# W2's Walsh-Hadamard transform: two more butterfly stages on GpSimd, and gates as one activation, in a mixer and gated FFN

## The chip, the cores and the metric

The kernel runs on one core of a Trainium2 chip. A core has TensorE (PE in the profile; PEld is its weight load), VectorE (DVE), ScalarE (ACT), GpSimd (POOL) and SyncE (SP, which here issues all DMAs). The metric is device microseconds of one execution, as the median of the runs. Before the change it is 731.81 us, the median of 3 runs from 729.76 to 732.04.

## The reference, cut to what matters

Input x is 4 blocks (batch) of 512 tokens of 512 values, float32.

```python
def attn(x, Wi, Wf, Wg, Wo, gnorm_w):          # weights 512 x 512
    i, f, g = x @ Wi.T, x @ Wf.T, x @ Wg.T
    gate = sigmoid(f)
    v = silu(i) * (1 - gate)
    o = scan over tokens of  o[t] = gate[t] * o[t-1] + v[t]
    o = o * rsqrt(mean(o*o) + 1e-5) * gnorm_w * silu(g)
    return o @ Wo.T
def ffn(x, W1, W2, W3):                        # W1, W3: 2048 x 512, W2: 512 x 2048
    hidden = silu(x @ W1.T) * (x @ W3.T)
    hidden = fwht(hidden)                      # Walsh-Hadamard over 2048, / sqrt(2048)
    return hidden @ W2.T
x = x + layernorm(attn(layernorm(x), ...))
x = x + layernorm(ffn(layernorm(x), ...))
```

## The kernel before, in words

The transform is put on W2 once, and not on the hidden values of each block: 2048 is 16 chunks of 128, so the transform is a 128 x 128 Hadamard product inside each chunk and a 16-point butterfly (four stages) across the chunks. W2 comes in 8 units of 64 output columns; a unit is 128 partitions x 16 chunks x 64 float32. GpSimd does three of the four stages (`FW.m.k`, unit m, k from 0 to 5: two instructions of 128x512 a stage, one for the sums and one for the differences, L1393 to L1407), going back and forth between the unit's place and a spare buffer (`unit_tmp`: x1r, gate or a half of ot, which units share in turn, so that a unit waits until TensorE has read the one before it in the same buffer). The fourth stage is on TensorE: for each half unit (`H2.m.h`, L746 to L756) two float32 products of 128 x 512 accumulate, with the Hadamard matrix and, for the second half, with its negative. A float32 product of this kind stands in the trace as two matmul records. ACT copies the bank to a float16 high half (L982), VectorE writes the float16 low half (L1298). All large products are of this kind: float16 high and low halves in three passes (`three_passes`, L580 to L582).

The work of a block b: `XT` transposes of the normed input; `F`, `I`, `G` projections (4 chunks c each; 12 matmuls of 512 columns a chunk); gates (below); the scan on VectorE (`S`, L1135 to L1144); squares of o summed on GpSimd (`S` there, L1373); low halves of the gated o on GpSimd (`P`, L1378); `MS` mean squares and `Y` output projection (4 tiles) on TensorE; norm, add, second norm (`YN`, `Z1`, `Z2`); `ZT` transposes; the FFN; the down projection `D.b.0` to `D.b.63` (chunk and token tile, three matmuls of 512 each); final norm `V` and `W`. Block 0's FFN is 16 chunks of `GA` and `UP` products (12 matmuls each). Blocks 1 to 3 use a scheme of seven products for a 2 x 2 grid in place of eight (`GP`, `GQ`, `GR`, `GU`, with `combine` steps on VectorE), whose sums of weights are made in blocks 0 and 1: raw weights are loaded (`SL`), summed by four GpSimd instructions (`SA`, L1419 to L1428), split (`SH` on ACT, `SO` on VectorE, L1246) and stored (`SS`); the next chunk of raw weights is loaded only when the last one is split.

A gate is a sigmoid on ACT, and then, for a silu, a product with the argument on VectorE: `I` L1132, `G` L1149, `GA` L1317. Then `UP` multiplies by the linear part (L1329), ACT makes the high half (L1009) and GpSimd the low half (`UP` there, L1432), which frees the buffer (`sga`, two deep) for the next-but-one gate.

What each engine does next is written out by hand in five lists: PE_ORDER (with the PSUM bank behind each colon), ACT_ORDER, DVE_ORDER, POOL_ORDER and SP_ORDER; each engine takes its list strictly in order, and semaphores make it wait for the others. The first down step waits for all low halves of W2 (`h2_lo`, L821).

## Time and profile before

| | us |
|---|---|
| median of 3 runs | 731.81 (729.76 to 732.04) |
| the profiled execution | 732.31 |
| its span, first to last instruction | 730.5 |
| TensorE busy | 702.2 (96%) |
| VectorE busy | 524.1 (72%) |
| GpSimd busy | 319.2 (44%) |
| ScalarE busy | 279.7 (38%) |
| mean granted TensorE clock | 0.988 |

Busy time is the union of an engine's instructions. Matmuls are pipelined, so how long one record is says less than how far apart two of them start. The full clock is 2.4 GHz and stands as 1.00; the lower level, 1.2 GHz, as 0.50. In a row of the timeline the first two numbers are the start and the length in us, then engine, line, operation, what it writes and reads, shape and count; in brackets the idle time before it and what ended that.

### The profile page before, as it was taken

How to read it: one execution, taken by the hardware profiler on the slowest of the kernel's cores; microseconds unless marked ns; L12 is line 12 of the kernel's file. 1: busy time of each engine (PE TensorE's matmuls, PEld its weight loads, DVE VectorE, ACT ScalarE, POOL GpSimd, SP SyncE). 2: the span in 40 equal slices, each digit the busy share in tenths (PEclk: the TensorE clock that was granted, in tenths of full speed). 3: DMA queues.
4: the chain of work that ended last, by engine and by line, in shares of the span. 5: the costliest groups of instructions: out<-in, count | busy, mean ns of one | idle time of the engine just before them, and what ended most of it. 6: DMA issues, size and time to landing. Idle time of an engine off the chain costs nothing.

```text
span 730.5 us, 11286 instructions
## 1 busy us (share of the span) xinstructions
PE 702.2 (96%) x4280; PEld 428.7 (59%) x4280; DVE 524.1 (72%) x873; ACT 279.7 (38%) x450; POOL 319.2 (44%) x268
## 2 busy tenths in 40 slices
...
GB/s 321 404 318 0 174 44 75 102 184 116 153 107 130 258 174 98 238 213 128 119 201 117 102 260 100 36 154 145 100 100 112 146 150 61 143 287 102 32 1 87
DMA packets 28199, 105.73 MB, mean 145 GB/s; under 512 B 2800, under 2 KB 7152, under 8 KB 23536
## 3 DMA queue, kind: packets, MB, share of 16 engines
...
HBM read 81.92 MB, written 23.07 MB: 144 GB/s over the span
## 4 chain that ended last, share of the span: by engine, by line
PE 69%; POOL 13%; DVE 7%; DMA 5%; issue 3%; ACT 2%; DVEq 1%; SPq 0%; POOLq 0%; ACTq 0%
PE ps L580 22%; PE ps L581 22%; PE ps L582 22%; DMA ring<-W13t 3%; DVE ring L1246 2%; POOL w2t L1407 2%; POOL ot L1407 2%; POOL ring L1432 1%; POOL ring L1422 1%; DMA ring<-L_attn_Wf 1%; POOL ring L1424 1%; POOL res L1417 1%; PE ps L722 1%; POOL x1r L1407 1%; POOL ring L1426 1%
## 5 line engine op out<-in xcount | busy, mean ns | idle before, releaser
L580 PE MATMUL ps<-xb,ring 128*128 128x256 f16 (+1 forms) x704 | 225.9, 321 | 1.4 <-DVE ring L1090 1.4
L581 PE MATMUL ps<-xb,ring 128*128 128x256 f16 (+1 forms) x704 | 225.9, 321 | 0.0
L582 PE MATMUL ps<-xb,ring 128*128 128x256 f16 (+1 forms) x704 | 225.9, 321 | 0.0
L1360 POOL TENSOR_TENSOR rstd<-var,neg_half 128x1 f32<-128x1 f32 x64 | 45.9, 718 | 120.7 <-DVE var L1338 55.1
L580 PEld LDWEIGHTS ps<-xb,ring 128*128 128x128 f16 x704 | 69.0, 98 | 48.2 <-issue 3.1
L581 PEld LDWEIGHTS ps<-xb,ring 128*128 128x128 f16 x704 | 68.9, 98 | 46.8 <-issue 1.7
L582 PEld LDWEIGHTS ps<-xb,ring 128*128 128x128 f16 x704 | 68.9, 98 | 42.1
L582 PE MATMUL ps<-ring 128*128 128x256 f16 x288 | 78.5, 273 | 0.0
L581 PE MATMUL ps<-ring 128*128 128x256 f16 x288 | 78.5, 273 | 0.0
L580 PE MATMUL ps<-ring 128*128 128x256 f16 x288 | 78.5, 273 | 0.0
L1432 POOL TENSOR_TENSOR ring<-sga,ring 128x512 f16<-128x512 f32 x36 | 45.6, 1280 | 71.7 <-ACT ring L1009 71.7
L1432 POOL TENSOR_TENSOR hsp<-sga,hsp 128x512 f16<-128x512 f32 x24 | 28.9, 1215 | 88.4 <-ACT hsp L1009 88.4
L1317 DVE SCALAR_TENSOR_TENSOR sga<-ring,gate_c,sga 128x512 f32<-128x512 f32 x48 | 41.1, 857 | 26.9 <-ACT sga L997 26.7
L976 ACT ACTIVATE junk<-ps 128x256 f32<-128x256 f32 x48 | 18.4, 383 | 96.7 <-PE ps L582 96.6
L580 PE MATMUL ps<-w2t,ring 128*128 128x512 f16 x144 | 54.6, 379 | 0.0
L581 PE MATMUL ps<-w2t,ring 128*128 128x512 f16 x144 | 54.6, 379 | 0.0
L582 PE MATMUL ps<-w2t,ring 128*128 128x512 f16 x144 | 54.6, 379 | 0.0
L997 ACT ACTIVATE sga<-ring,gate_c 128x512 f32<-128x512 f32 x48 | 34.6, 720 | 43.8 <-DVE ring L1281 35.3
L1270 DVE TENSOR_TENSOR ring<-ps,ring 128x512 f32<-128x512 f32 x48 | 33.0, 688 | 24.2 <-PE ps L582 23.7
L1281 DVE TENSOR_TENSOR ring<-ps,ring 128x512 f32<-128x512 f32 x48 | 33.1, 689 | 20.3 <-PE ps L582 19.5
L1260 DVE TENSOR_TENSOR ring<-ps,junk 128x512 f32<-128x512 f32 x48 | 33.1, 689 | 17.8 <-PE ps L582 15.0
L1378 POOL TENSOR_TENSOR ot<-sg,ot 128x512 f16<-128x512 f32 x16 | 22.4, 1397 | 50.9 <-ACT ot L916 50.9
...
## 6 DMA issues: line engine op xcount, KB each, us to landing
...
ring<-W13t SPq DMA_DIRECT2D x8, 1024.0 KB, 6.4
w_comb<-ring SPq DMA_DIRECT2D x8, 1024.0 KB, 8.5
...
w2t<-W2t SPq DMA_DIRECT2D x8, 512.0 KB, 11.6
...
```

The costliest lines, as they stand in the source:

```text
L580: pe.matmul(dst, a_hi, b_hi, start=start, stop=False)
L581: pe.matmul(dst, a_hi, b_lo, start=False, stop=False)
L582: return pe.matmul(dst, a_lo, b_hi, start=False, stop=stop)
L997: act.activation(sga[:, c % 2], src, ACT.Sigmoid, scale=gate_c[:]).then_inc(sga_rdy, 1)
L1260: dve.tensor_tensor(combined(g % 2)[:, 0:512].rearrange("p (o t) -> p o t", o=2), bank("GQ", b, g)[:].rearrange("p (o t) -> p o t", o=2), ...
L1270: dve.tensor_tensor(to[:, 512:1024].rearrange("p (o t) -> p o t", o=2), bank("GR", b, g)[:].rearrange("p (o t) -> p o t", o=2), both, ALU. ...
L1281: dve.tensor_tensor(to[:, 512:1024], bank("GU", b, g)[:], to[:, 512:1024], ALU.add).then_inc(gu_rdy, 1)
L1317: dve.scalar_tensor_tensor(sga[:, c % 2], src, gate_c[:], sga[:, c % 2], ALU.mult, ALU.mult).then_inc(sil_rdy, 1)
L1360: pool.tensor_tensor(dst, src, neg_half[:].broadcast_to(src.shape), ALU.pow).then_inc(done, 1)
L1378: pool.tensor_tensor(ot[:, 1, c, :], sg[:], ot[:, 0, c, :], ALU.subtract).then_inc(o_lo, 1)
L1407: pool.tensor_tensor(to, a, b, op).then_inc(w2_fly, 1)
L1432: pool.tensor_tensor(hid(b, c, 1), sga[:, c % 2], hid(b, c, 0), ALU.subtract).then_inc(hid_lo, 1)
```

## The change: what it does

1. All four stages of W2's butterfly run on GpSimd: 8 instructions a unit and not 6 (64, not 48, in all). They end in the unit's own place, with one spare buffer (x1r) for all units, and `FW` waits only for its own earlier steps. Each half unit is one product with the Hadamard matrix; the negative matrix and its step `HN` go. ACT's copy of a half now waits for both products of the unit, since its target overlaps their source. The first loads of x1r on SP wait for the last butterfly.
2. i, g and the FFN's gates are one Silu activation; the products on VectorE (`I`, `G`, `GA`) go, and the gain's coefficient goes into `P`, which becomes a scalar_tensor_tensor. The forget gate is 0.5 * tanh(f / 2) + 0.5: a Tanh and then an Identity on ACT. PSUM banks of `GA`, `I`, `G` are free after the activation.
3. Some small VectorE steps take another form: scalar_tensor_tensor on 128x1 becomes tensor_scalar, and three on 128x2 become pairs of 128x1.
4. All five order lists are new.

```diff
@@ butterflies and their product
-        def unit_tmp(m):
...
-        UNIT_TMP = ("x1r", "gate", "x1r", "ot0", "ot1", "gate", "x1r", "ot0")
...
+        unit_tmp = x1r[:].rearrange("p s d -> p (s d)").rearrange("p (c d) -> p c d", d=UW)
...
-            src, dst = (unit_raw(m), unit_tmp(m)) if stage % 2 == 0 else (unit_tmp(m), unit_raw(m))
+            src, dst = (unit_raw(m), unit_tmp) if stage % 2 == 0 else (unit_tmp, unit_raw(m))
...
-                pe.wait_ge(w2_fly, 6 * (m + 1))
...
-                pe.matmul(bank("H2", m, h)[:], had[:], low, start=True, stop=False)
-                pe.matmul(bank("H2", m, h)[:], neg_had[:] if h else had[:], high, start=False, stop=True
-                          ).then_inc(h2_mm, 1)
+                pe.wait_ge(w2_fly, 8 * (m + 1))
+                chunks = unit_raw(m)[:, HC // 2 * h:HC // 2 * (h + 1), :].rearrange("p c d -> p (c d)")
+                pe.matmul(bank("H2", m, h)[:], had[:], chunks, start=True, stop=True).then_inc(h2_mm, 1)
...
-                act.wait_ge(h2_mm, 2 * m + h + 1)
+                act.wait_ge(h2_mm, 2 * m + 2)
...
-                    sp.wait_ge(h2_mm, 2 * UNITS)
+                    sp.wait_ge(w2_fly, 8 * UNITS)
...
-                    if UNIT_TMP[m] == "gate":
-                        pool.wait_ge(o_rdy, KC)
-                    if UNIT_TMP[m] in ("ot0", "ot1"):
-                        pool.wait_ge(y_mm, TC)
-                    if unit_before(m) is not None:
-                        pool.wait_ge(h2_mm, 2 * (unit_before(m) + 1))
+                    if m > 0:
+                        pool.wait_ge(w2_fly, 8 * m)
@@ gates
-                act.activation(gate[:, c % 2], bank("F", b, c)[:], ACT.Sigmoid, scale=unscale[:, 0:1]
+                act.activation(gate[:, c % 2], bank("F", b, c)[:], ACT.Tanh, scale=unscale[:, 0:1]
+                               ).then_inc(tanh_rdy, 1)
+                act.wait_ge(tanh_rdy, n + 1)
+                act.activation(gate[:, c % 2], gate[:, c % 2], ACT.Identity, bias=half[:], scale=0.5
                                ).then_inc(gate_rdy, 1)
...
-                act.activation(si[:], bank("I", b, c)[:], ACT.Sigmoid, scale=unscale[:, 1:2]
+                act.activation(si[:], bank("I", b, c)[:], ACT.Silu, scale=unscale[:, 1:2]
...
-                act.activation(sga[:, c % 2], src, ACT.Sigmoid, scale=gate_c[:]
+                act.activation(sga[:, c % 2], src, ACT.Silu, scale=gate_c[:]
...
-                dve.scalar_tensor_tensor(si[:], bank("I", b, c)[:], unscale[:, 1:2], si[:],
-                                         ALU.mult, ALU.mult).then_inc(sli_rdy, 1)
...
-                dve.scalar_tensor_tensor(sg[:], bank("G", b, c)[:], g_coef[:, c:c + 1], sg[:],
-                                         ALU.mult, ALU.mult).then_inc(gs_rdy, 1)
...
-                dve.tensor_tensor(sg[:], sg[:], o_s[:], ALU.mult).then_inc(op_rdy, 1)
+                dve.scalar_tensor_tensor(sg[:], sg[:], g_coef[:, c:c + 1], o_s[:], ALU.mult, ALU.mult).then_inc(op_rdy, 1)
...
-                dve.scalar_tensor_tensor(sga[:, c % 2], src, gate_c[:], sga[:, c % 2],
-                                         ALU.mult, ALU.mult).then_inc(sil_rdy, 1)
@@ a small step's form
-                dve.scalar_tensor_tensor(var[:, 1, t:t + 1], mv[:, 1, t, 1:2], y_inv[:, 1:2], ms_eps[:, t:t + 1],
-                                         ALU.mult, ALU.add).then_inc(y_var, 1)
+                dve.tensor_scalar(var[:, 1, t:t + 1], mv[:, 1, t, 1:2], y_inv[:, 1:2], ms_eps[:, t:t + 1],
+                                  ALU.mult, ALU.add).then_inc(y_var, 1)
```

Of the new lists, the parts around the edits. PE_ORDER (up to block 0's first gate products, and from its last ones to the down projection):

```
... I.0.3:0 W2N.0.0:3 ... W2N.7.0 W2S.0.0:2 H2.0.0:1 MS.0.0:4 H2.0.1:5 Y.0.0:6 Y.0.1:0 WS.0.0:7 Y.0.2:3 Y.0.3:2
ZT.0.0:4 ZT.0.1:1 ZT.0.2:5 ZT.0.3:7 H2.1.0:6 H2.1.1:0 GA.0.0:3 XT.1.0:2 UP.0.0:4 XT.1.1:1 XT.1.2:5 XT.1.3:7 ...
... GA.0.14:6 UP.0.14:3 GA.0.15:2 UP.0.15:4 MS.1.0:0 Y.1.0:5 Y.1.1:1 Y.1.2:7 Y.1.3:6 H2.2.0:3 H2.2.1:2 H2.3.0:4
H2.3.1:0 H2.4.0:5 H2.4.1:1 H2.5.0:3 H2.5.1:7 H2.6.0:2 H2.6.1:4 H2.7.0:0 H2.7.1:5 D.0.0 D.0.1 D.0.2 D.0.3 D.0.4
D.0.5 ZT.1.0:7 ZT.1.1:4 D.0.6 D.0.7 D.0.8 ZT.1.2:5 ...
```

In the list before, H2.2 and H2.3 stand among the gate products of chunks 2 and 3, H2.4 to H2.7 around UP.0.12 ahead of block 1's projections. ACT_ORDER at the end of block 0's attention:

```
... S.0.2 WN.2.0 I.0.3 WN.3.0 P.0.2 WN.4.0 G.0.3 S.0.3 WN.5.0 P.0.3 WN.6.0 H2.0.0 H2.0.1 WN.7.0 WT.0.0 ...
```

POOL_ORDER (FW of units 0 and 1; then the end of the butterflies):

```
... X1.0.3 FW.0.0 FW.0.1 P.0.0 P.0.1 S.0.1 S.0.2 FW.0.2 FW.0.3 FW.0.4 P.0.2 FW.0.5 FW.0.6 FW.0.7 S.0.3 P.0.3
FW.1.0 FW.1.1 FW.1.2 Y.0.0 FW.1.3 Y.0.1 FW.1.4 FW.1.5 Y.0.2 YN.0.0 YN.0.1 Y.0.3 Z1.0.0 YN.0.2 YN.0.3 Z1.0.1
FW.1.6 Z1.0.2 Z1.0.3 FW.1.7 FW.2.0 X1.1.0 ...
... FW.6.7 UP.0.12 SA.1.0 P.1.0 S.1.1 FW.7.0 FW.7.1 FW.7.2 FW.7.3 FW.7.4 P.1.1 FW.7.5 FW.7.6 FW.7.7 P.1.2 S.1.2
SA.2.0 P.1.3 S.1.3 UP.0.13 UP.0.14 S.2.0 UP.0.15 Y.1.0 YN.1.0 Y.1.1 Y.1.2 Z1.1.0 YN.1.1 Y.1.3 YN.1.2 Z1.1.1
SA.3.0 Z1.1.2 YN.1.3 ...
```

DVE_ORDER at the end of W2 and at the end of the kernel; SP_ORDER around block 1's first combined weights:

```
... H2.7.0 H2.7.1 YN.1.3 Z2.1.1 Z1.1.2 SO.3.0 Z2.1.2 Z1.1.3 Z2.1.3 ZT.1.0 ...
... V.3.0 V.3.1 W.3.0 W.3.1 V.3.2 V.3.3 W.3.2 W.3.3
... SL.2.0 SS.1.0 LR.0.0 LR.0.1 WL.1.0 SL.3.0 SS.2.0 ST.1.0 ...
```

## Rows read from the trace of the kernel before

**Rows 1.** The page, part 1: busy us, share of the span, instructions

```profile
PE 702.2 (96%) x4280; PEld 428.7 (59%) x4280; DVE 524.1 (72%) x873; ACT 279.7 (38%) x450; POOL 319.2 (44%) x268
```

**Rows 2.** Table by stage, all engines; columns: stage, its us, busy, granted clock, DMA

```profile
52.00:91.00 39.00, 30.37 (x155) 16.87 (x153) 27.22 (x62) 19.31 (x32) 31.23 (x29) 0.82 0.30 103
91.00:166.80 75.80, 75.80 (x345) 35.32 (x344) 70.93 (x89) 39.40 (x62) 69.92 (x49) 1.00 0.28 98
...
183.10:218.00 34.90, 33.84 (x157) 15.18 (x155) 26.89 (x26) 17.19 (x26) 24.43 (x15) 1.00 0.41 135
...
248.00:260.00 12.00, 11.42 (x63) 5.95 (x62) 8.96 (x10) 6.38 (x11) 10.84 (x9) 1.00 0.63 209
260.00:724.00 464.00, 464.00 (x3200) 314.58 (x3198) 315.07 (x536) 140.06 (x234) 138.35 (x127) 1.00 0.37 131
```

**Rows 3.** Table by stage, GpSimd alone, then its butterflies (L1407) alone

```profile
84.00:216.00 132.00, 109.85 (x77) 0.98 0.36 122
...
84.00:216.00 132.00, 56.98 (x38) 0.98 0.36 122
```

**Rows 4.** Timeline of TensorE: output projection, transposes, Hadamard products, gate products, mean squares

```profile
59.79 0.59 PE L580 MATMUL ps<-ring,ot 128*128 128x512 f16 x1
...
81.45 1.09 PE L632 MATMUL ps<-ident,rows 128*128 128x128 f32 x4 [5.34 <-DVE rows L1186]
...
86.43 1.99 PE L754 MATMUL ps<-gate,had 128*128 128x512 f32 x2
...
90.83 0.38 PE L580 MATMUL ps<-xb,ring 128*128 128x512 f16 x1
...
166.78 1.02 PE L754 MATMUL ps<-ot,had 128*128 128x512 f32 x2
...
170.22 0.38 PE L580 MATMUL ps<-xb,ring 128*128 128x512 f16 x1
...
172.81 1.02 PE L754 MATMUL ps<-gate,had 128*128 128x512 f32 x2
...
218.10 1.02 PE L689 MATMUL ps<-ones,osum 128*128 128x1 f32 x8 [1.16 <-POOL osum L1373]
```

**Rows 5.** Timeline of GpSimd: the last add of squares, blocks 0 and 1

```profile
54.75 1.71 POOL L1373 TENSOR_TENSOR osum<-osum,osq 128x512 f32<-128x512 f32 x1
...
215.72 2.24 POOL L1373 TENSOR_TENSOR osum<-osum,osq 128x512 f32<-128x512 f32 x1
```

**Rows 6.** Line L1407, 84 to 216 us: least, median, greatest ns of one

```profile
L1407 POOL TENSOR_TENSOR x1r<-w2t x8: 1263/1714/1720, 86.2 to 149.5; 128x512 f32<-128x512 f32 x8
```

**Rows 7.** Groups by line: count, busy us, mean ns of one, idle before

```profile
L1317 DVE SCALAR_TENSOR_TENSOR sga<-ring,gate_c,sga 128x512 f32<-128x512 f32 x48 | 41.1, 857 | 26.9 <-ACT sga L997 26.7
L947 ACT ACTIVATE junk<-ring 128x1024 bf16<-128x1024 f32 x16 | 16.8, 1051 | 0.4
L1149 DVE SCALAR_TENSOR_TENSOR sg<-ps,g_coef,sg 128x512 f32<-128x512 f32 x16 | 11.8, 737 | 5.6 <-ACT sg L904 5.5
L1298 DVE SCALAR_TENSOR_TENSOR w2t<-ps,w_s,w2t 128x512 f16<-128x512 f32 x16 | 11.6, 746 | 5.6 <-ACT w2t L982 5.6
L1424 POOL TENSOR_TENSOR ring<-ring 128x512 f32<-128x512 f32 x8 | 10.8, 1350 | 0.6
L1338 DVE TENSOR_SCALAR var<-mv,v_inv 128x1 f32<-128x1 f32 x16 | 3.4, 214 | 0.7 <-DVE mv L1053 0.2
```

**Rows 8.** Timeline of VectorE: small steps of the first output norms

```profile
71.85 1.27 DVE L1167 SCALAR_TENSOR_TENSOR var<-mv,y_inv,ms_eps 128x1 f32<-128x1 f32 x1
...
73.29 0.16 DVE L1175 SCALAR_TENSOR_TENSOR ab<-mv,ysc 128x1 f32<-128x1 f32 x1
```

**Rows 9.** The page, part 6: DMA issues, KB each, us to landing

```profile
ring<-W13t SPq DMA_DIRECT2D x8, 1024.0 KB, 6.4
```

**Rows 10.** Timeline of ScalarE: the table load

```profile
0.73 1.28 ACT L839 ACT_TABLE_LOAD   x1 [0.73 <-PEq L1451]
```

**Rows 11.** The chain that ended last, its end

```profile
724.29 2.84 DMA x1r<-x_rows
```

More of the change, by code:

```diff
@@ L167 @@
[L167 to L171 removed]
+S.0.0 X1.0.0 X1.0.1 X1.0.2 X1.0.3 FW.0.0 FW.0.1 P.0.0 P.0.1 S.0.1 S.0.2 FW.0.2 FW.0.3 FW.0.4 P.0.2 FW.0.5 FW.0.6
@@ L213, in mixer_ffn_kernel @@
         neg_half = sb("neg_half", [P, 1])
+        half = sb("half", [P, 1])
         warm = sb("warm", [P, 1])
@@ L837, in _ @@
         def _(act):
-            act.wait_ge(half_set, 1)
-            act.activation(warm[:], neg_half[:], ACT.Sigmoid)
+            act.wait_ge(half_set, 2)
+            act.activation(warm[:], neg_half[:], ACT.Silu)
             def xt(b, t):
@@ L903, in g @@
                     act.wait_ge(o_lo, n)
-                act.activation(sg[:], bank("G", b, c)[:], ACT.Sigmoid, scale=unscale[:, 2:3]
+                act.activation(sg[:], bank("G", b, c)[:], ACT.Silu, scale=unscale[:, 2:3]
                                ).then_inc(sgg_rdy, 1)
@@ L1026, in _ @@
         def _(dve):
+            dve.memset(half[:], 0.5).then_inc(half_set, 1)
             dve.memset(neg_half[:], -0.5).then_inc(half_set, 1)
```

358 lines of the change are left out of this document (165 added, 193 removed).

## The prediction

> **What bounds the kernel now.** I read the page's busy shares first, then a table by stage, then TensorE's own order of time where the table shows a hole, then GpSimd the same way. TensorE is busy 96% of the span [rows 1]. A busy share says little by itself, because matmuls are pipelined, so look at the stages [rows 2]: from 91 to 166.8 us it is busy for 75.80 of 75.80 us, from 260 to 724 us for 464.00 of 464.00, at the full granted clock (1.00). In between it loses 1.1 us (183.1 to 218) and 0.6 (248 to 260). Only before 91 us are there real holes, 8.6 of 39 us at a granted clock of 0.82. So from the first gate product (90.83 us) to 724 us the time is TensorE's work plus 1.7 us, and an edit there counts only if it takes work from TensorE or makes it wait.
>
> The edge beside it is GpSimd from 84 to 216 us: busy for 109.85 of 132 us [rows 3]. It holds W2's butterflies, the hidden values' low halves, the sums of weights, and the low halves and squares of block 1's attention. The one wait of TensorE in that stage, 1.16 us in front of the mean squares at 218.10, ends with GpSimd's last add of squares (start 215.72) [rows 4, 5]. GpSimd has 22 us of slack there, and the change gives it more work. VectorE is at 70.93 of 75.80 us from 91 to 166.8 [rows 2], but nothing on TensorE waits for it.
>
> **1. One Hadamard product a half unit: TensorE.** Each half unit has two float32 products now, each of two records. Eight records take from 166.78 to 170.22, so 0.43 us each [rows 4]. Half of 64 records go: 32 x 0.43 = 13.7 us. They aren't worth the same. Unit 0's 1.7 us lie ahead of a hole of 5.34 us (the transposes at 81.45 wait for the rows) and are worth nothing. Unit 1's (86.43 to 90.83, part of it at half clock) lie between the transposes and the first gate product. Those of units 2 to 7, 24 records, 10.3 us, lie in the full stretch and come off whole: **-10.3 us**.
>
> **2. Two more butterflies a unit: GpSimd.** 16 instructions more. Mean of one now, 84 to 216 us: 56.98 / 38 = 1.50 us [rows 3]; the ends are 1.26 and 1.72 [rows 6]. That is 24 us, 20 to 27.5. What it costs depends on the cover, in three places.
>
> *(a) The front.* The new list puts five of unit 0's butterflies between the adds of squares 2 and 3, three of them right before the last; now only one stands there. Now the last add ends at 56.5 [rows 5] and the output projection starts at 59.79 [rows 4]. In the new ACT list each piece of weight squares (two passes of 1.05 us, some 2.3 us with their readings [rows 7]) precedes one of the last gates: WN.2, I, WN.3, P.0.2, WN.4, G.0.3, S.0.3, WN.5, P.0.3. From 48 us, where I put the first of them, I count 4 x 2.3 + 5 x 0.65 and 1.2 of waiting for the last I product = 13.7, so the last low half of o is there at about 62 + 1.3 = 63; Y starts near 64.5, not 59.8, but with unit 0's products already done. The stage's granted clock is 0.82 [rows 2]: part of it runs at 1.2 GHz and not 2.4, after TensorE had waited, and an output tile that falls there takes up to twice its 2.59 us. I put 2 us of that into Y here. Then Y.0.3 ends near 76; now it is 72.5 (81.45 less the hole of 5.34 and unit 0's products of 3.4). From there norm, add and second norm take until the transposes end at 86.4, 14 us, and in them small VectorE operations wait up to 1.27 us, where 0.16 is normal [rows 8]. The new forms (one scalar operand fewer, L1167 and L1175) don't need that wait if they behave as L1338, 0.21 on the mean of 16 [rows 7]. With three of four tiles already on their way I take 10 us for it: last transposes at 86, unit 1 then 1.7 to 3.4 us, **first gate product at 89.3, not 90.83: -1.5 us** (bounds 86.5 and 94).
>
> The Trainium skill ("SBUF — State Buffer", Who interferes with whom) has a rule for this: a VectorE operation with two inputs in SBUF and a GpSimd operation that reads SBUF exclude each other for a whole instruction. The trace agrees for the small operations (1.27 us against 0.16). By that rule added butterflies would also slow VectorE's weight splits; VectorE loses more work than that (part 3).
>
> *(b) 84 to 216 us.* By 86.3 us (unit 1's last butterfly as I count it) the new list has done 16 butterflies, the old one 10 by 84. So 10 of the 16 fall into the stage: 10 x 1.50 = +15.0. Of the sums of weights only three chunks, not four, stand ahead of the last add of squares: four instructions less, of some 1.35 to 1.43 (L1424 [rows 7]; I take 1.35) = -5.4. So 109.85 + 15.0 - 5.4 = 119.5 us from 86.3 on, end 205.8; with 2.5 us for waits that remain (now 22; the list puts its work in another order, and a chunk of raw weights lands 6.4 us after its issue [rows 9]) 208.3. TensorE has before the mean squares: 32 gate and up products and 12 projections, 44 x 2.59 (170.22 to 172.81 is one [rows 4]), and four short transposes and a little: 115.8, from 89.3 to 205.1. It waits 3.2 us where it now waits 1.2: **+2.0 us**. Bounds: no wait (-1.2) and, with nothing absorbed in the front and 1.72 each, 109.85 + 27.5 - 5.4 + 86.3 + 2.5 = 220.8, a wait of 15.7 (+14.5). I take the mean of the stage because the same 32 weight splits run beside GpSimd as now, and what comes on top runs after them, near 1.26.
>
> *(c) Units 2 to 7 in one piece before the down projection.* Now they stand among gate products. In the new list D.0.0 stands right behind H2.7.1 and waits for its copy on ACT (about the same 0.7) and its low half on VectorE (0.75 [rows 7]), with two handovers: **+1.7 us** (0.9 to 4; VectorE needs 0.75 a bank and TensorE will need 0.86, so it just keeps up). Behind it on VectorE and ACT stand block 1's last norm steps and one chunk of weight sums (two instructions on VectorE), while TensorE has 9 down steps (5.8 us) and two transposes before it needs the last norm: I put 1.6 us of waiting, against the 0.6 lost there now [rows 2]: **+1.0 us** (0 to 4).
>
> **3. Gates as one activation.** VectorE loses the multiplications by the argument: 48 x 0.86 and three sets of 16 x 0.74 = 77 us [rows 7]; P changes form, which I price at nothing. ACT keeps its number for i, g and the FFN gates and gains one 0.6 us step for each of 16 forget gates, 10 us on an engine 38% busy [rows 1]. In the full stretch nothing waits for these 77 us, so they are worth **0**; they shorten hand-offs and free banks sooner, which makes the stretch from 260 to 724 us safer. Behind a forget gate's extra step stands the scan, 0.6 us a chunk; in the front that is inside (a).
>
> **4. SP, POOL and the end.** The first two loads of x1r wait for the last butterfly instead of the last product; both come long before their use in block 0's final norm. In SP's list the first combined weights are asked for earlier and wait for the last up product (near 205), and raw chunk 3 queues behind; its sums are first read by block 1's combined products. The last order on VectorE is W.3.0 W.3.1 V.3.2, so W.3.1 and its load of x1r (issued at 724.29 now, a wait of 2.84 us [rows 11]) come one norm earlier: **-0.7 us**.
>
> Sum: -1.5 - 10.3 + 2.0 + 1.7 + 1.0 - 0.7 = **-7.8 us**. The profiled execution took 732.31 us (span 730.5, 1.8 around it), so 724.5; it stands 0.5 over the median of the runs (731.81), so **724.0** for the median.
>
> **The rivals.**
> 1. *TensorE keeps all it gains.* GpSimd is through before 205 us and the last units hide their copies. For it: 22 us of slack [rows 3], butterflies of 1.26 after the splits. Against: the order on GpSimd puts a chunk of sums (5.4 us) before the last P and S. -1.5 - 10.3 - 1.2 - 0.7 = -13.7: **718.1**.
> 2. *GpSimd becomes the bound up to the mean squares* (the other side). Place: S.1.3 at the end of its list. Price: each us past 205.1 is one of TensorE. It eats the gain once GpSimd ends 11 us after TensorE gets there (216), so at 119.5 + 8 us of work or waits. At the upper bound of (b): -7.8 + 12.5 = +4.7, **736.5**. For it: TensorE already ends its wait at 218 on just that instruction. Against: butterflies moved ahead of 86 us.
> 3. *The full stretch leaks.* Orders laid out anew put pairs of products in bunches over four banks; 0.03 us at each of their 144 bank hand-overs, or five waits of 1 us, make +5: **729**. For it: now 464.00 of 464.00, which can only get worse. Against: VectorE has 48 x 0.86 us less in just these hand-overs.
> 4. *The tables switch.* If Tanh and Silu aren't loaded together, each forget gate needs two loads, 32 x 1.28 = 41 us on ACT, of which block 0's 8 (10 us) lie on the path and the rest beside TensorE's work: -7.8 + 10 and some waits, **736**. The skill's page gives 2.66 us a switch with its drain; by that figure, an estimate, it would be 21 us.
>
> **How the numbers follow.** Forecast 0.47, rival 1 0.26, rival 2 0.13, rival 3 0.11, rival 4 0.03. A change under 0.3% (2.2 us: 729.6 to 734.0) can't be told from none here. Faster: 0.47 + 0.26 + 0.05 of rival 3 = 0.78. Same: 0.05 of rival 2, 0.05 of 3 = 0.10. Slower: 0.08 + 0.01 + 0.03 = 0.12. The likeliest one's own range is 721 to 728; to hold 8 in 10 it reaches from just under rival 1 to the near half of rivals 2 and 3: 716.5 to 730.
>
> **What would show it.** Step 1: 32 records on the line of the Hadamard product, none on a second. (a): the first gate product between 88 and 91 us, Y from about 64. (b): GpSimd's last add of block 1 near 208 and a wait of TensorE of 2 to 5 us before the mean squares; no wait makes rival 1, over 10 us rival 2. (c): a hole of 1 to 2.5 us between the last Hadamard product and the first down step. Step 3: one table load and no more; over 260 to 724 us TensorE busy throughout. Wrong would be the whole argument if the end moves by more than TensorE's work plus the holes of its own timeline.

## The result and the profile after

The changed kernel takes 736.38 us (median of 5 runs, 735.30 to 737.85) where the kernel before takes 731.81 (729.76 to 732.04). The ratio is 1.0072, 95% interval 1.0050 to 1.0094: slower, by 0.7%. I had forecast 724.0 (716.5 to 730). Of all executions here only one is far from its median: one of the six of e13_front_and_fill took 1883.9 us, and its ratio leaves that one out.

The page of after, part 1, beside [rows 1]; columns as there:

```profile
PE 692.5 (94%) x4248; PEld 424.9 (58%) x4248; DVE 463.1 (63%) x781; ACT 291.6 (40%) x466; POOL 335.4 (46%) x284
```

TensorE has lost 32 instructions, as the change says. VectorE has lost 61 us, and not the 77 of my step 3. The span is 734.6 us, 4.1 more than before: TensorE does less and waits longer. Where, the table by stage says (columns as in [rows 2]):

```profile
52.00:91.00 39.00, 23.09 (x105) 12.80 (x102) 23.23 (x63) 21.42 (x37) 31.93 (x29) 0.73 0.15 51
91.00:166.80 75.80, 75.51 (x350) 35.07 (x349) 68.01 (x75) 37.84 (x59) 72.25 (x52) 0.98 0.34 113
...
183.10:218.00 34.90, 27.95 (x131) 12.69 (x128) 22.36 (x14) 15.99 (x24) 34.19 (x24) 0.93 0.38 128
218.00:232.00 14.00, 14.00 (x57) 6.81 (x57) 8.61 (x21) 2.17 (x4) 8.15 (x8) 0.81 0.54 169
232.00:248.00 16.00, 13.58 (x41) 5.83 (x40) 15.21 (x29) 11.67 (x17) 10.77 (x11) 1.00 0.09 34
...
260.00:728.00 468.00, 468.00 (x3221) 316.47 (x3219) 266.48 (x476) 148.56 (x245) 138.32 (x131) 1.00 0.38 134
```

From 260 us on TensorE is busy for 468.00 of 468.00, as before. From 183.1 to 218 it is busy for 27.95 of 34.9 where it was 33.84, and GpSimd, which had 24.43 us of work there, has 34.19. TensorE's timeline of after names the waits (start, us, engine, line, operation, and in brackets the idle time ahead and its releaser):

```profile
83.77 1.09 PE L617 MATMUL ps<-ident,rows 128*128 128x128 f32 x4 [5.24 <-DVE rows L1154]
88.64 3.01 PE L617 MATMUL ps<-ident,rows 128*128 128x128 f32 x12 [3.79 <-DVE rows L1154]
91.45 2.89 PE L737 MATMUL ps<-w2t,had 128*128 128x512 f32 x4
94.28 0.38 PE L565 MATMUL ps<-xb,ring 128*128 128x512 f16 x1
...
217.69 1.84 PE L674 MATMUL ps<-ones,osum 128*128 128x1 f32 x8 [6.95 <-POOL osum L1338]
219.39 0.59 PE L565 MATMUL ps<-ring,ot 128*128 128x512 f16 x1
...
244.49 0.38 PE L565 MATMUL ps<-w2t,hsp 128*128 128x512 f16 x1 [2.42 <-DVE w2t L1274]
...
252.32 0.63 PE L707 MATMUL ps<-ident,rows 128*128 128x128 f32 x4 [0.97 <-DVE rows L1154]
```

The 1.16 us in front of block 1's mean squares [rows 4] have become 6.95, and the releaser is the same: GpSimd's last add of squares. The wait costs more than itself, since the granted clock is down behind it; the same line read in two windows (stage, TensorE busy, granted clock, DMA):

```profile
212.94:223.18 10.24, 5.49 (x17) 0.50 0.50 165
223.18:226.00 2.82, 2.82 (x15) 1.00 0.94 286
```

0.50 is 1.2 GHz, 1.00 is 2.4. The mean squares and the first output tile lie in the slow window and take 1.7 and 4.4 us where they take 0.9 and 2.6 at full clock: 2.6 us more. GpSimd's timeline shows what it did ahead of that add:

```profile
190.61 2.25 POOL L1368 TENSOR_TENSOR x1r<-w2t 128x512 f32<-128x512 f32 x1
...
202.98 2.82 POOL L1368 TENSOR_TENSOR w2t<-x1r 128x512 f32<-128x512 f32 x2
205.76 1.60 POOL L1343 TENSOR_TENSOR ot<-sg,ot 128x512 f16<-128x512 f32 x1
207.33 2.18 POOL L1338 TENSOR_TENSOR osum<-osum,osq 128x512 f32<-128x512 f32 x1
209.47 1.71 POOL L1383 TENSOR_TENSOR ring<-ring 128x512 f32<-128x512 f32 x1
...
215.16 1.16 POOL L1343 TENSOR_TENSOR ot<-sg,ot 128x512 f16<-128x512 f32 x1
216.28 1.27 POOL L1338 TENSOR_TENSOR osum<-osum,osq 128x512 f32<-128x512 f32 x1
```

It hardly ever pauses: of the 34.90 us from 183.1 to 218 it is busy for 34.19. Counted from the end of unit 1's last butterfly to the end of that add, all of GpSimd and then its butterflies alone:

```profile
90.15:217.55 127.40, 122.85 (x85) 0.97 0.36 122
...
90.15:217.55 127.40, 75.57 (x48) 0.97 0.36 122
```

The queue is also one half of a chain through other engines: the last two `G` gates of block 1 on ScalarE wait for GpSimd's low half before them, and VectorE's product waits for the first of these gates:

```profile
201.77 0.69 ACT L886 ACTIVATE sg<-ps,unscale 128x512 f32<-128x512 f32 x1 [1.61 <-POOL ot L1343]
...
202.49 0.96 DVE L1124 SCALAR_TENSOR_TENSOR sg<-sg,g_coef,o_s 128x512 f32<-128x512 f32 x1 [2.99 <-ACT sg L886]
...
207.46 0.69 ACT L886 ACTIVATE sg<-ps,unscale 128x512 f32<-128x512 f32 x1 [2.77 <-POOL ot L1343]
```

TensorE's last record, before and after:

```profile
723.96 0.38 PE L582 MATMUL ps<-w2t,xb 128*128 128x512 f16 x1
```

```profile
728.43 0.38 PE L567 MATMUL ps<-w2t,xb 128*128 128x512 f16 x1
```

The groups by line of after (count, busy us, mean ns), and for the weight splits (L1216) the same group of before (L1240), which [rows 7] does not hold:

```profile
L1368 POOL TENSOR_TENSOR w2t<-x1r 128x512 f32<-128x512 f32 x32 | 49.2, 1556 | 3.2 <-PE ps L722 2.4
L1368 POOL TENSOR_TENSOR x1r<-w2t 128x512 f32<-128x512 f32 x32 | 48.5, 1531 | 22.9 <-DMA w2t<-W2t 21.8
L1216 DVE SCALAR_TENSOR_TENSOR ring<-ring,w_s 128x512 f16<-128x512 f32 x32 | 48.1, 1557 | 0.0
...
L1135 DVE TENSOR_SCALAR var<-mv,y_inv,ms_eps 128x1 f32<-128x1 f32 x16 | 4.4, 273 | 0.8 <-DVE mv L1034 0.2
```

```profile
L1240 DVE SCALAR_TENSOR_TENSOR ring<-ring,w_s 128x512 f16<-128x512 f32 x32 | 41.2, 1308 | 0.0
```

### The profile page after: what moved, and what is told of

Read it like the earlier page. It is cut to its first block, busy times and chain, and to the rows that moved or that the text cites. A ratio compares the mean times of both kernels' runs of the same rounds, so it can differ in the third digit from the quotient of the medians.

```text
span 734.6 us, 11163 instructions
## 1 busy us (share of the span) xinstructions
PE 692.5 (94%) x4248; PEld 424.9 (58%) x4248; DVE 463.1 (63%) x781; ACT 291.6 (40%) x466; POOL 335.4 (46%) x284
## 4 chain that ended last, share of the span: by engine, by line
PE 73%; POOL 11%; DVE 11%; issue 2%; DMA 1%; DVEq 1%; ACT 0%; SPq 0%; POOLq 0%
PE ps L565 23%; PE ps L566 23%; PE ps L567 23%; DVE ring L1216 5%; POOL w2t L1368 3%; POOL x1r L1368 2%; PE ps L707 1%; POOL ring L1393 1%; POOL rstd L1325 1%; DVEq L1033 1%; POOL ring L1389 1%; POOL ring L1383 1%; DVE sga L1294 1%; PE ps L617 1%; POOL ring L1387 1%
## 5 line engine op out<-in xcount | busy, mean ns | idle before, releaser
L1325 POOL TENSOR_TENSOR rstd<-var,neg_half 128x1 f32<-128x1 f32 x64 | 42.9, 672 | 98.9 <-DVE var L1303 29.8
L567 PE MATMUL ps<-ring 128*128 128x256 f16 x288 | 78.5, 273 | 0.0
L566 PE MATMUL ps<-ring 128*128 128x256 f16 x288 | 78.5, 273 | 0.0
L565 PE MATMUL ps<-ring 128*128 128x256 f16 x288 | 78.5, 273 | 0.0
L1368 POOL TENSOR_TENSOR x1r<-w2t 128x512 f32<-128x512 f32 x32 | 48.5, 1531 | 22.9 <-DMA w2t<-W2t 21.8
L1294 DVE SCALAR_TENSOR_TENSOR sga<-ring,up_c,sga 128x512 f32<-128x512 f32 x48 | 39.2, 820 | 24.2 <-ACT sga L977 22.3
L1368 POOL TENSOR_TENSOR w2t<-x1r 128x512 f32<-128x512 f32 x32 | 49.2, 1556 | 3.2 <-PE ps L722 2.4
L1216 DVE SCALAR_TENSOR_TENSOR ring<-ring,w_s 128x512 f16<-128x512 f32 x32 | 48.1, 1557 | 0.0
```

What stands on the lines that cost most here:

```text
L565: pe.matmul(dst, a_hi, b_hi, start=start, stop=False)
L566: pe.matmul(dst, a_hi, b_lo, start=False, stop=False)
L567: return pe.matmul(dst, a_lo, b_hi, start=False, stop=stop)
L1216: dve.scalar_tensor_tensor(ffn_w(c)[:, w, 1], ffn_raw(c)[:, w], w_s[:, w:w + 1], ffn_w(c)[:, w, 0], ALU.mult, ALU.subtract).then_inc(wt_lo, 1)
L1294: dve.scalar_tensor_tensor(sga[:, c % 2], src, up_c[:], sga[:, c % 2], ALU.mult, ALU.mult).then_inc(hid_rdy, 1)
L1325: pool.tensor_tensor(dst, src, neg_half[:].broadcast_to(src.shape), ALU.pow).then_inc(done, 1)
```

## The experiments

All were run beside the kernel before. Ratio to it, with its 95% interval; the last two columns are TensorE's start, in each profile, of block 1's mean squares and of the first down product (left empty for e4, whose order of TensorE is that of before).

| kernel | us | ratio | mean squares | first down |
|---|---|---|---|---|
| after | 736.38 | 1.0072 (1.0050 to 1.0094) | 217.7 | 244.5 |
| e1_pool_swap | 735.48 | 1.0052 (1.0037 to 1.0066) | 214.9 | 243.0 |
| e2_h2_in_hole | 736.27 | 1.0061 (1.0045 to 1.0077) | 222.2 | 233.4 |
| e3_small_last | 724.94 | 0.9909 (0.9891 to 0.9926) | 209.0 | 233.1 |
| e4_gates_alone | 732.89 | 1.0024 (1.0010 to 1.0038) | | |
| e5_middle | 755.68 | 1.0333 (1.0309 to 1.0358) | 215.4 | 251.9 |
| e6_front | 742.17 | 1.0148 (1.0121 to 1.0175) | 224.6 | 251.5 |
| e7_both | 759.34 | 1.0386 (1.0361 to 1.0412) | 219.8 | 256.3 |
| e8_swap_clean | 739.39 | 1.0112 (1.0097 to 1.0128) | 216.3 | 248.2 |
| e9_swap_fill | 736.81 | 1.0083 (1.0069 to 1.0097) | 214.8 | 243.2 |
| e10_attention_first | 734.64 | 1.0061 (1.0048 to 1.0074) | 211.2 | 242.6 |
| e11_sums_back | 734.20 | 1.0042 (1.0028 to 1.0056) | 212.0 | 236.1 |
| e12_sums_late | 732.46 | 1.0020 (1.0010 to 1.0030) | 211.4 | 235.4 |
| e13_front_and_fill | 737.32 | 1.0089 (1.0065 to 1.0112) | 215.7 | 237.4 |
| e14_front_norm | 738.04 | 1.0094 (1.0073 to 1.0114) | 217.7 | 245.2 |

**Is it GpSimd's work?** e3_small_last:

```diff
+            if stage == 3:
+                return d[:, :, half, 0:64], s[:, :, 0, 0:64], s[:, :, 1, 0:64], ALU.subtract if half else ALU.add
```

> The kernel after with the fourth butterfly stage computed on 64 of the 512 elements of each partition (seven eighths of that stage are left out); the number of instructions and all orders stay. It takes away GpSimd's time for 16 of the 64 butterflies' halves, some 16 x 1.3 = 21 us, 14 of them ahead of the mean squares. Theory A (GpSimd's added work costs the result): the wait ahead of the mean squares goes (7.1 us), with it the half clock (2.6), and a part of the front's 3.5: 9 to 13 us off, 723.5 to 727.5. Theory B (it is the order of the steps, not GpSimd's work): under 3 us, 733.5 to 736.5.

724.94 us, 11.4 under after. No order was touched, and TensorE now meets its square in time; TensorE's mean squares, GpSimd's last add, the shortened butterflies and VectorE's splits in its trace:

```profile
208.98 1.02 PE L676 MATMUL ps<-ones,osum 128*128 128x1 f32 x8
...
207.57 1.27 POOL L1340 TENSOR_TENSOR osum<-osum,osq 128x512 f32<-128x512 f32 x1
...
L1370 POOL TENSOR_TENSOR w2t<-x1r 128x512 f32<-128x512 f32 x16 | 25.7, 1623 | 2.7 <-PE ps L724 2.4
L1370 POOL TENSOR_TENSOR w2t<-x1r 128x64 f32<-128x64 f32 x16 | 7.5, 484 | 0.5
...
L1218 DVE SCALAR_TENSOR_TENSOR ring<-ring,w_s 128x512 f16<-128x512 f32 x32 | 41.0, 1337 | 0.0
```

This is theory A. 8.7 us earlier at the mean squares and 2.6 of half clock make the 11.4. The splits are back at 1337 ns with nothing of theirs changed. The 0.9% under before is no kernel to keep, since most of a stage is missing; it shows what is left of the 10.3 us of step 1 where GpSimd isn't in the way, but the front (first gate product at 93.2 us, 90.83 before) and the wait at the first down product (2.42 us) still cost.

**Are the gates worth nothing?** e4_gates_alone is before with `ACT.Silu` for i, g and the FFN gates, and `ACT.Tanh` with `ACT.Identity, bias=half, scale=0.5` for f; VectorE's order without I, G and GA.

> The kernel before with its butterflies, products and orders, and only the gates changed to one activation each (Silu, and Tanh with a second step for the forget gate); VectorE's order loses the steps I, G and GA. Theory A (my step 3: VectorE's 77 us stand beside TensorE and are worth nothing): 731 to 733 (731.8 before). Theory B (they shorten the front and the last wait of the middle stage): up to 3 us off, 729. Theory C (the gates themselves cost, by the extra ScalarE step or by tables): 734 or more.

732.89 us, inside theory A's range, but by the interval 0.7 to 2.8 us over the kernel before that ran beside it (731.08). The gates are worth nothing, or cost up to 0.4%; where that little comes from stays open.

**Can TensorE's wait be ordered away?** e1 moves one chunk of sums behind the last low half and square, e2 puts ready Hadamard products into TensorE's wait:

```diff
-P.1.2 S.1.2 SA.2.0 P.1.3 S.1.3          (e1, POOL_ORDER)
+P.1.2 S.1.2 P.1.3 S.1.3 SA.2.0
-UP.0.15 MS.1.0 Y.1.0 ... Y.1.3 H2.2.0 ... H2.7.1   (e2, PE_ORDER, banks changed)
+UP.0.15 H2.2.0 ... H2.7.1 MS.1.0 Y.1.0 ... Y.1.3
```

> The kernel after with one step of GpSimd's order moved: SA.2.0, a chunk of weight sums of four instructions (5.7 us in the trace of after), stands behind the last two low halves and squares of block 1's attention and no longer ahead of them. Theory A (GpSimd is what TensorE waits for up to block 1's mean squares, and its order decides when): the mean squares at 217.7 us come at about 212.3, TensorE's wait of 7.1 us shrinks to 1.7, and the stretch at half clock behind it (1.2 GHz from 212.9 us, some 2.6 us more of TensorE) shrinks or goes: 5 to 8 us off, 728.5 to 731.5. Theory B (the loss sits elsewhere, in the front or in the down projection, and the wait only stands in for it): under 1.5 us, 735 to 736.5.

> The kernel after with the twelve Hadamard products of units 2 to 7 ahead of block 1's mean squares and output projection on TensorE instead of behind them (their copies and low halves on ScalarE and VectorE go with them, and the down products of block 0 are spread otherwise between the transposes that follow). GpSimd's order is untouched. Theory A (TensorE idles 7 us for GpSimd, and 10 us of ready work stood behind the wait): the wait at 210.6 us is filled, the clock stays up, and the bubble before the first down product (2.6 us) goes too: 9 to 11.5 us off, 725 to 727.5. Theory B (the units aren't ready any earlier, or what is gained is waited for again at the last norm of block 1): 0 to 4 us off, 732.5 to 736.5.

0.9 and 0.1 us, both theory B by the time. In e2 the first down product starts 11.1 us earlier, as forecast, and the gain is given back by 290 us. TensorE's wait and the step on VectorE that stands ahead of the norm it waits for:

```profile
252.81 1.09 PE L709 MATMUL ps<-ident,rows 128*128 128x128 f32 x4 [4.76 <-DVE rows L1156]
...
246.53 2.48 DVE L1224 SCALAR_TENSOR_TENSOR ring<-ring,w_s 128x1024 f16<-128x1024 f32 x2 [3.98 <-ACT ring L949]
```

VectorE is to write the norm's rows, and stands at a weight-sum step that waits for ScalarE, which waits for GpSimd. In e1 the mean squares came 2.8 us earlier and not 5.4: with the sums out of the way GpSimd stood idle for 2.41 us ahead of the last low half (212.38 us), which needs ScalarE's copy. Behind the mean squares the same weight-sum step stood on VectorE ahead of their reading (it waited 8.65 us, until 221.22), and the FFN's last gate came on ScalarE at 222.65 us, behind that chunk's split and the low half UP.0.13, both of which the swap had left late.

Two larger rearrangements, and both together, came out much worse. e5 moves the weight sums behind block 1's norm and puts units 2 and 3 ahead of the mean squares; e6 puts the output projection ahead of unit 0's products and GpSimd's last low halves and square ahead of unit 0's last butterflies, and so moves butterflies of units 0 and 1 back; e7 is both. Their orders for PE and POOL, cut:

```diff
-UP.0.15 MS.1.0 Y.1.0 ... Y.1.3 H2.2.0 ...        (e5, PE_ORDER, banks changed)
+UP.0.15 H2.2.0 H2.2.1 H2.3.0 H2.3.1 MS.1.0 Y.1.0 ... Y.1.3 H2.4.0 ...
-... Z1.1.1 SA.3.0 Z1.1.2 ... ZA.1.6 SA.4.0 X1.2.0 ...   (e5, POOL_ORDER)
+... Z1.1.1 Z1.1.2 ... ZA.1.6 SA.3.0 X1.2.0 ...
-FW.0.2 FW.0.3 FW.0.4 P.0.2 FW.0.5 FW.0.6 FW.0.7 S.0.3 P.0.3 FW.1.0 FW.1.1 FW.1.2 Y.0.0 ...   (e6, POOL_ORDER)
+P.0.2 FW.0.2 FW.0.3 S.0.3 P.0.3 FW.0.4 FW.0.5 Y.0.0 FW.0.6 Y.0.1 FW.0.7 FW.1.0 Y.0.2 ...
```

> The kernel after with new orders in the middle only (front and all arithmetic as in after): units 2 and 3 ahead of block 1's mean squares on TensorE and units 4 to 7 behind the output projection; on GpSimd the last two low halves and squares ahead of a chunk of weight sums; the next chunks of weight sums behind block 1's norm and no longer inside it (VectorE's steps and the loads on SP with them); the down products of block 0 spread to match. Why: filling TensorE's wait alone gave nothing, because in that trace the norm of block 1 stood behind VectorE's step on the weight sums (it waited 4.0 us for GpSimd's) and TensorE then waited 4.9 us at the norm's transposes and 3.6 us at block 2's. Theory A (the loss is GpSimd's wait, and after it a second and third wait of the same kind, all three a matter of order): the first down product at 233.5 us and not 244.5, no wait over 1 us behind it: 11 to 12.5 us off, 723.5 to 726. Theory B (behind the two waits stands a third resource, such as VectorE at 12 to 13 of 14 us there): 3 to 8 us off, 728 to 733.

> The kernel after with new orders in the front only (up to 110 us): the output projection ahead of unit 0's Hadamard products, GpSimd's low half and squares of the last gates ahead of unit 0's last butterflies, ScalarE's copies of the last gates ahead of the weight squares, unit 1's products behind the first gate and up product. Theory A (GpSimd bounds the stretch up to the mean squares of block 1 whatever TensorE does ahead of it): the first gate product comes 6 to 8 us earlier (86 to 88 us, 94.3 in after), but the mean squares only 0 to 3 us, so 0 to 3 us off: 733 to 736. Theory B (the front's delay of 3.5 us over the kernel before goes straight into the end): 6 to 8 us off, 728 to 730.

> Both sets of orders together. Theory A: the middle's 11 us, and of the front's 6 to 8 us what GpSimd lets through. TensorE then comes to the mean squares near 208 us and GpSimd's last add of squares ends near 213: 720 to 723. Theory B of the front (all of it counts): 716.5 to 719. If the middle's orders only work because TensorE comes late to them: 725 or more.

All three lie above every range given for them but e7's last, which is open upwards. TensorE waits in e5 for 3.41 us behind the mean squares, for a gate on ScalarE that waits 7.97 us for UP.0.13 behind the sums on GpSimd; then 7.81 and 3.36 us at the Hadamard products and the first down product, where VectorE is late with its low halves behind two weight-sum steps (229.62 us, 3.48 long) and the norm; and 9.57 us in block 2, whose gates on ScalarE stand behind chunk 6 of the sums (GpSimd starts it at 314.2 us, 289.5 in after). e6 is the cleaner lesson: its first gate product came at 95.1 us, not at 86 to 88, and the mean squares 6.9 us later than in after. TensorE's wait there, and GpSimd from 90 us:

```profile
224.63 1.62 PE L677 MATMUL ps<-ones,osum 128*128 128x1 f32 x7 [9.29 <-POOL osum L1341]
...
90.00:224.00 134.00, 129.04 (x90) 0.95 0.35 116
```

Butterflies moved out of the front come back at the mean squares: theory A's mechanism, with a worse end than either theory had. The first gate product came 0.8 us later than in after, so this isn't a test of what an earlier TensorE would bring.

**Amount or place?** e8 is e1 with UP.0.13 in GpSimd's idle time and the later steps on the sums behind the first norm steps; e9 adds two units' products ahead of the mean squares; e10 takes the other way: block 1's attention steps first on GpSimd, unit 7's butterflies between and behind them, the same work. On ScalarE and VectorE e10 also puts the steps on the sums behind the gates.

```diff
-UP.0.12 SA.1.0 P.1.0 S.1.1 FW.7.0 ... FW.7.4 P.1.1 FW.7.5 FW.7.6 FW.7.7 P.1.2 S.1.2 SA.2.0 P.1.3 S.1.3 UP.0.13 ...
+UP.0.12 FW.7.0 P.1.0 SA.1.0 S.1.1 P.1.1 FW.7.1 FW.7.2 S.1.2 P.1.2 FW.7.3 FW.7.4 FW.7.5 S.1.3 P.1.3 UP.0.13 SA.2.0 ...
```

> The swap of e1 (last low half and squares of block 1 ahead of the chunk of weight sums) mended: in e1's trace the last gate product's copy on ScalarE still waited for GpSimd's low half UP.0.13, which that order had put behind the sums, and VectorE's step on the sums stood ahead of the mean squares. Here GpSimd does UP.0.13 in its 2.4 us gap, and both steps on the sums come behind the first norm steps. Theory A (GpSimd is the bound up to the mean squares): they come at 213 to 215 us (217.7 in after), VectorE no longer holds the norm behind them, 3.5 to 6 us off: 730.5 to 733. Theory B (behind GpSimd VectorE is just as full from 218 to 246 us, so nothing is gained): 0 to 1.5 us off, 735 to 736.5.

> The kernel e8_swap_clean with the four Hadamard products of units 2 and 3 (3.4 us) in TensorE's wait ahead of the mean squares, and the down products spread to match. Theory A: wait and half clock both go, and VectorE is eased by 3 us behind the output projection: 8 to 10.5 us off against after, 726 to 728.5. Theory B (the norm of block 1 ends no earlier and TensorE waits at its transposes instead): 3.5 to 6 off, 730.5 to 733.

> The kernel after with block 1's attention steps put first on GpSimd: unit 7's butterflies behind or between them (two behind the last square), a chunk of weight sums behind the first low half, and ScalarE's and VectorE's steps on the sums behind the gate they held up. In after's trace the first low half of block 1 starts at 188.3 us though its input was there at 182.7, and each gate on ScalarE waits for GpSimd's low half before it, down to the last square at 216.3. GpSimd's work is the same. Theory A (it is not the amount of GpSimd's work but the place of the attention's steps in its queue that TensorE waits for): the last square ends by 209, TensorE reaches the mean squares at 210.6 and doesn't wait, clock stays up: 9 to 11 us off, 725.5 to 727.5. Theory B (the amount: what is moved behind comes late for the Hadamard products or the norm): 3 to 6 us off, 730.5 to 733.5.

e8 and e9 came out above their theory B: the mean squares came 1.4 and 2.9 us earlier than in after, and TensorE then waited among the Hadamard products (3.1 and 5.95 us) for VectorE's low halves and, in e8, ScalarE's rows. e10: theory A for the mean squares, but the time lies above both ranges. TensorE's mean squares come without a wait, and what they gained goes in the next 20 us; TensorE, GpSimd and VectorE in its trace:

```profile
211.17 0.95 PE L675 MATMUL ps<-ones,osum 128*128 128x1 f32 x8
...
229.77 1.61 PE L738 MATMUL ps<-w2t,had 128*128 128x512 f32 x2 [2.98 <-ACT rows L901]
...
220.09 0.55 POOL L1326 TENSOR_TENSOR rstd<-var,neg_half 128x1 f32<-128x1 f32 x1
...
220.67 0.21 DVE L1141 TENSOR_SCALAR ysc<-rstd,y_inv 128x1 f32<-128x1 f32 x1 [4.22 <-POOL rstd L1326]
221.05 4.10 DVE L1223 SCALAR_TENSOR_TENSOR ring<-ring,w_s 128x1024 f16<-128x1024 f32 x2
```

The first norm's variance is there at 216.45; its root waits 3.6 us in GpSimd's queue, and then the sums take VectorE for 4.1. e11 (to e10) puts each chunk of sums from 2 on in the next one's place and the first norm's steps earlier on GpSimd; e12 (to e11) loads chunk 3 earlier and does chunk 6 earlier on VectorE, so that chunk 7 lands sooner:

```diff
-... UP.0.13 SA.2.0 UP.0.14 ... Z1.1.1 SA.3.0 Z1.1.2 ...    (e11, POOL_ORDER; SH, SO, SL, SS likewise)
+... UP.0.13 FW.7.6 FW.7.7 Y.1.0 UP.0.14 ... Z1.1.1 SA.2.0 Z1.1.2 ...
-ST.1.2 ST.1.3 SL.3.0 SS.2.0        (e12, SP_ORDER)
+ST.1.2 SL.3.0 SS.2.0 ST.1.3
-S.2.2 SO.6.0 P.2.2                 (e12, DVE_ORDER)
+SO.6.0 S.2.2 P.2.2
```

> e10_attention_first with the chunks 2 to 7 of weight sums each in the next chunk's place on GpSimd, ScalarE, VectorE and SP. In e10's trace TensorE reached the mean squares without a wait (211.2 us, 217.7 in after), but 5 of the 9 us gained came back as waits among the Hadamard products: GpSimd took up the first norm's root 3.7 us late (chunk 2 of the sums and the last low halves stood before it), and VectorE's two steps on the sums (4.1 us) stood between the first and the second norm. Theory A (the order can hide the added butterflies; the sums are what is in the way twice): the first down product at 234.5 to 236 us (244.5 in after, 242.6 in e10), no new wait over 1 us up to 320, at most 2.5 us at the combined weights near 335: 7 to 9.5 us off against after, 727 to 729.5, which is faster than the kernel before by a little. Theory B (VectorE and GpSimd are full from 212 to 246 us whatever stands where): 234 to 235.

> e11_sums_back with two steps changed: the load of chunk 3 on SP ahead of the last store of block 1's rows, and VectorE's step on chunk 6 ahead of the third scan of block 2. In e11's trace the middle gave what was forecast (first down product at 236.1 us, 244.5 in after; block 2's first gate at 281.5, 289.4), but chunk 7 came late: its load landed at 317.5 us, GpSimd's sums ran until 323.6 with block 2's last square behind them, and TensorE waited 3.4 us at the mean squares (325.0) and 1.8 more behind them, part of it at half clock. Theory A (the delay is the chunks' chain alone): chunk 7 lands some 4 us earlier, the wait at block 2's mean squares falls under 1 us: 4.5 to 7 us off against e11, 727 to 729.7, under the kernel before. Theory B (the scan moved behind takes the place of the sums): 732 to 735.

e11's trace, TensorE and then GpSimd:

```profile
236.10 0.38 PE L566 MATMUL ps<-w2t,hsp 128*128 128x512 f16 x1 [2.42 <-DVE w2t L1275]
...
325.00 1.02 PE L675 MATMUL ps<-ones,osum 128*128 128x1 f32 x8 [3.19 <-POOL osum L1339]
...
317.55 1.74 POOL L1384 TENSOR_TENSOR ring<-ring 128x512 f32<-128x512 f32 x1 [2.71 <-DMA ring<-W13t]
...
323.60 1.26 POOL L1339 TENSOR_TENSOR osum<-osum,osq 128x512 f32<-128x512 f32 x1
```

The first down product is nearly where theory A had it (236.1, from 244.5), the time where theory B had it: a load that now lands at 317.5 us holds the same kind of square in block 2. e12 cuts that wait to 1.61 us and takes off 1.7 us of the 4.5 to 7 forecast: theory B by the time. It stands at 732.46, 3.9 us under after and by 0.20% (0.10 to 0.30) over before. No version with the whole computation beats before.

**Does the front count?** e14 takes two weight splits on VectorE (and two weight copies on ScalarE) out from between block 0's last transposes; e13 does that on e12's orders, with two units' products ahead of the mean squares.

```diff
-Z2.0.0 WT.0.1 WT.1.0 Z1.0.2 ... Z2.0.3 ZT.0.0 X1.1.0 ZT.0.1 ZT.0.2 ZT.0.3 X2.1.0     (DVE_ORDER)
+Z2.0.0 Z1.0.2 ... Z2.0.3 ZT.0.0 X1.1.0 ZT.0.1 ZT.0.2 ZT.0.3 WT.0.1 WT.1.0 X2.1.0
-WT.2.0 ZT.0.0 WT.2.1 ZT.0.1 ZT.0.2 ZT.0.3 H2.1.0 H2.1.1      (ACT_ORDER)
+ZT.0.0 ZT.0.1 ZT.0.2 ZT.0.3 WT.2.0 H2.1.0 H2.1.1 WT.2.1
```

> The kernel after with two weight splits of VectorE (WT.0.1, WT.1.0) and two weight copies of ScalarE behind the last three transposes of block 0's norm and no longer between them (TensorE waits 4.1 us there, from 84.4 us). The first gate product should come 2.5 to 4 us earlier than 94.3. Theory A (up to the mean squares GpSimd's queue is the bound, a late TensorE costs nothing): the mean squares stay within 1.5 us of 217.7 and the time within 1.5 us of after's: 735 to 737. Theory B (the front's delay goes into the end): 732.5 to 734.

> e12_sums_late with the front's edit of e14_front_norm, and the four Hadamard products of units 2 and 3 ahead of the mean squares, so that a TensorE that comes 3.5 us earlier doesn't wait for GpSimd's last square. Theory A (with GpSimd's order mended the front counts, 2.5 to 3.5 us): 729 to 730.5, level with the kernel before or under it. Theory B (the chunks' chain is fixed by other engines, so that what TensorE wins it waits for at block 2's mean squares): 731.5 to 733.

In e14 the first gate product starts at 92.2 us, 2.1 earlier than in after, the mean squares at

```profile
217.68 1.62 PE L675 MATMUL ps<-ones,osum 128*128 128x1 f32 x7 [6.97 <-POOL osum L1339]
```

against 217.69. That is theory A for the mean squares; the time, 738.04, lies above both ranges. But TensorE also waited at the next block's transposes (95.7 to 101.8 us) and reached the end of the up products no earlier than in after, so this shows that the front's edit was taken back at once, by VectorE; it doesn't show what a truly earlier TensorE would bring. What it lost against after (1.2 us by the start of the last transpose of block 1's norm, 261.8 and 260.6 us) it lost behind the mean squares, and why is open. e13 came out above both its ranges. Its first gate product is 0.7 us earlier than in e12 (94.3, 95.1), its first down product 2.0 us later (237.4, 235.4), and block 2's mean squares, with 2.99 us of wait for GpSimd's square, 4.3 us later (326.5, 322.2). Its fill and its front weren't tried apart.

## Why the prediction was wrong, step by step

**Step 1, the products.** 10.3 us in the full stretch: right. There are 32 records of the Hadamard product, on one line. From the first gate product to the last record TensorE takes 633.1 us before and 634.2 after; less its waits (1.7; 6.95 + 2.42 + 0.97 + 0.3) and the 2.6 us of half clock that is 631.4 and 620.9, 10.5 apart.

**Step 2 (b), GpSimd from 84 to 216 us, is the step that failed.** I had it end at 208.3; it ended at 217.55, 9.25 later, and the mean squares came at 217.69 and not at 208.3. Term by term: unit 1's last butterfly ended at 90.15 and not 86.3 (+3.85); the work behind it was 122.85 us and not 119.5 (+3.35), the butterflies alone more than that, 48 at 1.574 us where I took 1.50 (+3.6); and idle time was 4.55 and not 2.5 (+2.05). I had bounded this by 220.8 and let the mean of a freer GpSimd stand, because "the same 32 weight splits run beside GpSimd as now". They do, but the two engines slow each other: the splits went from 1308 to 1557 ns and are back at 1337 in e3, and the butterfly at 190.61 us, beside VectorE's weight-sum step, took 2.25 us where one beside an idle VectorE took 1.26 (65.64 us). Nor were 1.26 and 1.72 the ends before, as I read [rows 6]: those are eight of the stage's 38 butterflies, and another took 2.12 us (163.21 us), also beside VectorE's weight-sum step. The Trainium skill ("SBUF — State Buffer", Who interferes with whom) states the rule for both directions: the port pair that the two engines share is an exclusive lock, and the order in which the two instructions issue decides which of them waits. The trace agrees, with these numbers. I cited it for VectorE and did not apply it to GpSimd. The +3.85 us came in from the front, where that butterfly stands between steps of the late norm; so 3.85 of the 9.25 us are (a)'s error carried into GpSimd's queue.

TensorE's own side of the sum held: from the first gate product to its wait for the mean squares it took 116.3 us, 115.8 forecast. What I left out altogether is the clock behind the wait: 2.6 us.

**The list hid a worse thing than the amount.** I counted GpSimd's queue as a sum with one end. In it block 1's low halves release ScalarE's next gate, which releases VectorE's product, and so the copy that the next low half needs; e10 gives the mean squares without a wait with the same 64 butterflies. That the place of these steps decides when TensorE gets its square is shown, for the three queues together: e10 also moved the steps on the sums on ScalarE and VectorE, and the shares weren't tried apart. So both are true: with this order the work is too much (e3), and with another order the same work is in time there (e10). That order alone gives back the whole isn't shown: e12 recovers 3.9 us of some 12.

**Step 2 (a), the front.** -1.5 forecast, +3.5 measured: the first gate product at 94.28. Y came at 66.2 for 64.5 and ended at 78.5 for 76, and the last transposes ended at 91.65, not 86. The term that was most wrong is the norm behind Y: 13.1 us where I took 10 (14 before). VectorE's rows wait behind two weight splits, 3.79 us on TensorE, where before it was 0.83; e14, with these splits moved, has 2.21 and 0.36. The small steps behaved as I said (L1135 at 273 ns).

**Step 2 (c), units 2 to 7 in one piece.** 1.7 us forecast for the bubble at the first down product, 2.42 measured; 1.6 for the wait at the last norm, 0.97 measured. Right in kind and nearly in size.

**Step 3, the gates.** One table load of 1.28 us and no second, 468.00 of 468.00 busy: rivals 3 and 4 are out. Worth 0 or a little less by e4. The 77 us of products did go, but VectorE's own splits took 6.9 us more and `P` in its new form 2.9 more, which I had priced at nothing; with smaller changes elsewhere the net is 61.

**Step 4, the end.** 0.7 us forecast, 0.4 measured: from the start of TensorE's last record to the end of the span 6.5 us before, 6.2 after.

**The rivals.** Rival 2, GpSimd as the bound up to the mean squares, is what happened, at nearly its price (736.5; 736.38 measured). That the price fits is in part luck: it had the mean squares at 220.8 and no half clock, and they came at 217.7 with 2.6 us of it. Its point of decision, a wait of 11 us, was wrong: 7 us of wait did it, because TensorE came late as well and the clock fell behind the wait. Rival 1 rested on GpSimd's 22 us of idle time [rows 3]: added work used it up (4.55 us are left) and still ended late.

From the forecast to the result: 724.0 + 9.4 (the mean squares) + 2.6 (half clock) + 0.7 (bubble) - 0.6 (last norm) + 0.3 (the end) = 736.4, measured 736.38. The fit is good to half a microsecond, not better: the forecast took off 0.5 us because the profiled execution of before lies that much above its median, and that of after is its median.
